# Inverse norms of q and k: from two GpSimd powers per pair to ten Vector instructions in the last product's PSUM bank

## What is computed

```python
qkv = x @ Wqkv                       # 128 -> 3 * 1024, 16 heads of 64
q = l2norm(q) * qs;  k = l2norm(k) * ksc
q = q * cos * scale + rotate_half(q) * sin * scale
k = k * cos / scale + rotate_half(k) * sin / scale
out = local_attention(q, k, v)       # windows of 32 rows, each sees itself and the one before
x = out @ Wo + x                     # then the feed-forward part, in the same manner
```

## Time and profile before

| what | us |
|---|---|
| median of 3 runs | 5035.57 (5034.55 to 5038.77) |
| profiled execution | 5033.9 |
| its span | 5032.1 |
| busy in the span: PE / DVE / ACT / POOL | 4258.0 / 2925.1 / 2870.9 / 3317.2 |
| L915, the power, 192 times | 1044.1 |
| one round (p2, p3, p0, p1 in the stretch 3006.11 to 3173.61) | 39.66 + 38.71 + 50.55 + 38.58 |

### The profile page before, as it was taken

The page is one execution under the profiler, slowest core; times in us unless marked ns, Lnnn a source line. Parts: engine busy times, 40 slices in busy tenths (PEclk is TensorE's granted clock), DMA queues, the critical chain, the costliest instruction groups (busy, mean ns, idle before and its releaser), DMA issues. The chain is left out here.

```text
span 5032.1 us, 165624 instructions
## 1 busy us (share of the span) xinstructions
PE 4258.0 (85%) x68354; PEld 2963.6 (59%) x68806; DVE 2925.1 (58%) x4217; ACT 2870.9 (57%) x4801; POOL 3317.2 (66%) x1514
## 2 busy tenths in 40 slices
PE   5878878688888888888888888888888888888884
PEld 2434444366666666666666666666666666666663
DVE  6565665565655565556555655565556555655564
ACT  2534445356665666666656666666666566655662
POOL 0000000588788888888788888888888888888882
PEclk9988989799999999999999999999999999999997
DMA  0000000222222222222222212222222122212222
GB/s 26 3 14 15 3 15 2 59 55 65 60 53 61 65 60 53 61 65 60 53 61 65 60 53 61 65 60 53 61 65 60 53 61 65 60 53 61 65 60 76
DMA packets 284570, 259.23 MB, mean 52 GB/s; under 512 B 122871, under 2 KB 258508, under 8 KB 271148
## 3 DMA queue, kind: packets, MB, share of 16 engines
q1 hardware_dynamic: 283820, 248.14, 18.3%
HBM read 117.63 MB, written 29.77 MB: 29 GB/s over the span
## 5 line engine op out<-in xcount | busy, mean ns | idle before, releaser
L790 DVE TENSOR_TENSOR products<-bank_d,table 128x1024 f32<-128x1024 f32 x772 | 937.6, 1215 | 787.5 <-ACT sq L606 751.9
L910 POOL TENSOR_TENSOR products<-products 128x2048 f32<-128x2048 f32 x192 | 870.5, 4534 | 373.7 <-DVE products L790 373.6
L915 POOL TENSOR_TENSOR rnorm<-clamped,minus_half 128x32 f32<-128x32 f32 x192 | 1044.1, 5438 | 16.0
L393 PE MATMUL bank_d<-w_qkv,xT 128*128 128x512 f32 x1544 | 832.0, 632 | 9.9 <-DVE products L790 8.5
L606 ACT ACTIVATE sq<-bank_d 128x512 f32<-128x512 f32 x772 | 467.8, 606 | 531.5 <-PE bank_d L393 521.6
L788 DVE TENSOR_REDUCE ss<-sq 128x16 f32<-128x1024 f32 x386 | 469.6, 1217 | 455.4 <-ACT sq L606 455.4
L933 POOL TENSOR_TENSOR qk_rot<-products,rnorm 128x2048 f32<-128x2048 f32 x192 | 695.4, 3622 | 14.9 <-POOL rnorm L915 14.0
L877 POOL MEMSET ident<- 128x128 f32 x1 | 0.2, 205 | 915.2 <-POOLq L1051 915.2
L462 PE MATMUL scores<-kT,qT 64*32 64x64 f32 x24576 | 424.2, 218 | 141.9 <-issue 79.5
L940 POOL TENSOR_TENSOR prob<-prob,inv_sum 128x1024 f32<-128x1024 f32 x192 | 365.0, 1901 | 261.8 <-DVE inv_sum L770 261.8
L435 PE MATMUL bank_a<-ident,qk_rot 128*128 128x128 f32 x3072 | 423.5, 293 | 116.5 <-issue 107.7
(11 more groups left out here) (160 smaller groups left out, 7647.4 us busy)
## 6 DMA issues: line engine op xcount, KB each, us to landing
v_back<-v SPq DMA_DIRECT2D x96, 768.0 KB, 5.4
w_qkv<-in_Wqkv_dram SPq DMA_DIRECT2D x25, 1024.0 KB, 5.0
v_back<-v SPq DMA_DIRECT2D x192, 128.0 KB, 5.5
w_qkv<-in_Wqkv_dram SPq DMA_DIRECT2D x25, 512.0 KB, 5.2
xs<-x_layers SPq DMA_DIRECT2D x194, 64.0 KB, 2.0
w_o<-in_Wo_dram SPq DMA_DIRECT2D x24, 512.0 KB, 5.8
xr<-x_layers SPq DMA_DIRECT2D x96, 128.0 KB, 3.1
x<-x SPq DMA_DIRECT2D x96, 128.0 KB, 1.8
```

What stands on the lines that cost most here:

```text
L393: nc.tensor.matmul(bank[:, :], xT[:, P * a:P * (a + 1)], w_qkv[:, col:col + 512], start=True, stop=True).then_inc(d_filled if i < 8 else a ...
L790: nc.vector.tensor_tensor(products[:, a, head:head + 8, :, :].rearrange("p h r (o d) -> p h r o d", o=2), bank[:, :].rearrange("p (h r d) ...
L910: link(nc.gpsimd.tensor_tensor(products[:, a, :, 0, :], products[:, a, :, 0, :], products[:, a, :, 1, :], ALU.add))
L915: link(nc.gpsimd.tensor_tensor(rnorm[:, a, :], clamped[:, a, :], minus_half[:, :], ALU.pow))
```

## The change

The clamp and the power leave GpSimd. DVE computes all 64 inverse roots of a pair at once, behind the product of chunk 7: a first guess by integer arithmetic on the bits, one step of third order and one Newton step. The intermediate values x, t and u lie in the first 192 columns of the bank that chunk 7 was in, y and w in SBUF. Each of the ten instructions waits for the one before through the semaphore `v_link`, and the first also for the product. `d_free` of chunk 7 is raised by the tenth instruction in place of the product. The last one also waits for `qk_ready` of the pair before, since it overwrites `rnorm`. On POOL `norm_qk(s, 0)` moves from between the two `normalise` to behind both and behind the wait for chunk 7.

```diff
                 head = HEADS * kq + 8 * c
-                nc.vector.tensor_tensor(
+                product = nc.vector.tensor_tensor(
...
-                    ALU.mult).then_inc(d_free, 1)
+                    ALU.mult)
+                if i == 7:
+                    link(product)
+                    inverse_norms(pair, bank).then_inc(d_free, 1)
+                else:
+                    product.then_inc(d_free, 1)
+
+            def inverse_norms(pair, bank):
+
+                x, t, u = (bank[:, 4 * HEADS * k:4 * HEADS * (k + 1)] for k in range(3))
+                y, w = root_y[:, :], root_u[:, :]
+                link(nc.vector.tensor_scalar(x, ss[:, :, :].rearrange("p a h -> p (a h)"), FLT_MAX, 1e-24, ALU.min, ALU.max))
+                link(nc.vector.tensor_scalar(y.bitcast(i32), x.bitcast(i32), -0.5, float(RSQRT_MAGIC), ALU.mult, ALU.add))
+                link(nc.vector.tensor_tensor(t, x, y, ALU.mult))
+                link(nc.vector.tensor_tensor(t, t, y, ALU.mult))
+                link(nc.vector.tensor_scalar(w, t, 0.375, -1.25, ALU.mult, ALU.add))
+                link(nc.vector.tensor_tensor(u, t, w, ALU.mult))
+                link(nc.vector.scalar_tensor_tensor(y, u, 1.875, y, ALU.add, ALU.mult))
+                link(nc.vector.tensor_tensor(t, x, y, ALU.mult))
+                link(nc.vector.scalar_tensor_tensor(t, t, -0.5, y, ALU.mult, ALU.mult))
+
+                if later(pair.n):
+                    dve.wait_ge(qk_ready, 2 * pair.n)
+                return nc.vector.scalar_tensor_tensor(rnorm[:, :, :].rearrange("p a h -> p (a h)"), t, 1.5, y, ALU.add, ALU.mult)
...
-            def inverse_norms(a):
-
-                link(nc.gpsimd.tensor_scalar(clamped[:, a, :], ss[:, a, :], FLT_MAX, 1e-24, ALU.min, ALU.max))
-                link(nc.gpsimd.tensor_tensor(rnorm[:, a, :], clamped[:, a, :], minus_half[:, :], ALU.pow))
...
                     add_products(s, 0)
-                    inverse_norms(0)
                 if runs(back3):
                     normalise_x1(back3)
                 if runs(back1):
                     normalise(back1, 0)
-                if runs(now):
-                    norm_qk(s, 0)
-                if runs(back1):
                     normalise(back1, 1)
                 if runs(now):
                     pool.wait_ge(d_free, chunk_at(now, 7)[1] + 1)
+                    norm_qk(s, 0)
                     if s.p == POS - 1:
                         make_table(s.f + 1)
                     add_products(s, 1)
-                    inverse_norms(1)
                     norm_qk(s, 1)
```

More of the change, by code:

```diff
@@ L148, in local_layers @@
         rnorm = sb("rnorm", [P, 2, 2 * HEADS])
-        clamped = sb("clamped", [P, 2, 2 * HEADS])
-        minus_half = sb("minus_half", [P, 2 * HEADS])
+        root_y = sb("root_y", [P, 4 * HEADS])
+        root_u = sb("root_u", [P, 4 * HEADS])
+        minus_half = sb("minus_half", [P, 2])
         epsilon = sb("epsilon", [P, 2])
@@ L921, in normalise_x1 @@
                 nc.gpsimd.tensor_scalar(neg_mean[:, :], mean_var[:, :, 0], -1.0, 1.0, ALU.mult, ALU.mult)
-                link(nc.gpsimd.tensor_tensor(rstd[:, :], var_eps[:, :], minus_half[:, 0:2], ALU.pow))
+                link(nc.gpsimd.tensor_tensor(rstd[:, :], var_eps[:, :], minus_half[:, :], ALU.pow))
                 for a in range(2):
```

## The result

The changed kernel takes 5230.3 us (median of 4 runs, 5227.6 to 5236.1) against 5037.2 us (4 runs) before: ratio 1.0384, 95% interval [1.0366, 1.0402]. The profiled execution has a span of 5225.5 us, 193.4 us more than before. The forecast was 5166 us, + 132 us, with a range of 5085 to 5240.

The account below looks back on a forecast made before the run. PE's own work and a few waits were taken to bound the kernel. 1.62 + 1.53 + 1.6 + 0.8 = 5.55 us a round, 128 us in 23 rounds, plus 4 us for the first, gave 5166 us; range 5085 to 5240.

Parts of the forecast that it names:

- What bounds the kernel: Whole step: PE's own work and a few waits set the pace; POOL's busy time is worth nothing by itself.
- The power leaves POOL: At p1 to p3 PE's 1.65 us wait for xn goes, but only 0.3 us come through, yT being next.
- The cost D: Ten DVE instructions between the product of chunk 7 and the row sum take 2.65 us, bounds 2.1 to 3.3.
- The choice to add nothing for the bank: The ten instructions on DVE: PSUM source costs no more than SBUF; the skill's table would add 0.6 us.
- The shift of a step: PE's transposes for ph = 1 start later, waiting for prob: 1.62 us at p1, 1.53 p2, 1.6 p3, 1.95 p0.
- p0 and the holes: PE's 2.4 us hole at p0, read as code loading behind v_back: p0 taken as + 0.8 us.
- the lower of the two ends: At p0 the new wait replaces PE's hole and the clock stays up: -2.2 us; the other end is + 1.95.
- The clock: PE's clock falls behind the new wait, 1.7 us each fall: 5330 us if in each step; chance 0.10.
- The table at p3: At p3 the table makes DVE's rotate 0 of the new pair 2.2 us late, 53 us more: 5219; chance 0.09.
- The other side: In three steps of each round PE keeps 0.3 us if the insertion costs below 0.8 us: 5012 us; chance 0.04.

Follow-up runs that it names:

- the experiment with only the ten instructions: Kernel before with the ten instructions added on DVE, result unread, POOL keeping its clamps and powers: 5225.1 us, ratio 1.0390.
- the two held kernels: v_back loaded behind times_v: the kernel before with only that, 4955.3 us; the changed kernel with that and the ten instructions behind the row sum, 4932.2 us.
- without the roots: Changed kernel with one clamp written to rnorm in place of the ten instructions, q and k scaled wrongly: 4989.1 us, ratio 0.9912.

## Why the prediction was right, and where it was short

**What bounds the kernel.** Right. PE's list and its few waits set each step; POOL lost a third of its busy time and this changed nothing in the loop, as the experiment with only the ten instructions shows most plainly. The exception is the first round, which the prediction didn't look at for this: there the kernels without the power on POOL are 10.5 to 11.6 us faster than their partners with it (140.2 against 128.7 and 129.7, 141.5 against 129.9, and 149.7 with only the ten against 138.9 with the change).

**The power leaves POOL.** Right in kind: of the 1.65 us for `xn` most went into the waits for `gate` and `yT`, 0.6 us each. At p1 0.33 us come through without the roots (38.58 to 38.25), 0.17 with them behind the row sum (38.41), and 0.12 between the two held kernels (38.59 to 38.47). So 0.3 us a step is the upper end, and that the two held kernels are 23 us apart doesn't show it, as worked out above.

**The cost D.** 2.65 us foretold, 2.63 measured. The straight line between two rows was as good as the row itself. The choice to add nothing for the bank was off by 0.12 us of the chain.

**The shift of a step.** Right: with `v_back` held the transposes for ph = 1 begin 1.59, 1.50 and 1.58 us later at p1, p2 and p3, against 1.62, 1.53 and 1.6 foretold, and 1.57 at p0 against 1.95. In the sum it is 7.0 us a round, against 1.62 + 1.53 + 1.6 + 1.95 = 6.7 us worked out with the full shift at p0, so 160.5 us in all. That the sums are so near is luck in part, since by steps p1 took 0.6 us more and p3 and p0 together 0.2 us less.

**p0 and the holes.** Here the forecast was short, by 61 us. The step that failed is the one that set this aside for p0 alone. I had seen that `v_back` would be issued at another moment against PE, named it as the likely cause of the hole at p0, and then asked only what this does to p0. There it did what was foretold in kind: p3 and p0 together rose by 0.8 us instead of 2.4. Counted on PE, p3 rose by 1.9 us, about as foretold, and p0 fell by 1.0: its holes in `times_v` went from 2.70 to 1.20 us a round and its mean granted clock from 0.895 to 0.932, so it went part of the way to the lower of the two ends that the prediction kept. But at p1, where there had been no hole, the later transposes and the nearer load put a packet of PE's code 2.9 us behind the issue of `v_back`, and opened one: + 6.3 us instead of + 1.6, a term of 4.7 x 23 = 108 us that the sum doesn't have. Holding the load takes 4.0 of the 4.7 us away. What it had too much of was 1.6 us at p0 and p3, 37 us. With 2 us of p2, and the first round and the two ends of the program, which came 11 to 12 us lower than counted, the difference is the 61 us.

**The rivals.** The clock did not fall behind the wait for `prob` (1.00 at p1 and p2 in the rounds without a long hole); it fell behind the new hole at p1 in some rounds (mean of the step down to 0.93). The table at p3 did make rotate 0 of the new pair late, by 8.77 us of idle time against 5.29, and this did not show in the step. What the prediction did not ask is what the table does to `qk_rot` of tile 1, which POOL makes behind it: at the end of p3 PE now waits for it in 17 of 23 rounds, 2.0 us in the mean of all. It cost nothing to speak of, as a hole of 2.5 us had been at that place before.

**The other side.** The gain that stays was given D below 0.8 us. The same gain is had without touching D, by standing behind the row sum; that is the case that I should have priced beside it.

## What to carry to other kernels

A chain of small instructions is cheap or dear by what stands behind it in its engine's list: look for the first instruction behind it that another engine waits for, take its slack from the trace, and if the chain is longer, move it behind that instruction. Relieving an engine that nobody waits for gives only what the one wait on it gave, less what stands next in line; look apart at the first steps, where the pipeline fills and another engine can be the one that all wait for. And where a change shifts engines against SP, look at the big loads in every step, not only in the step that has a hole already: where a load lies against dense PE code is worth testing by one held wait.

## What the runs showed of the hardware that I had not expected

- PE's dense stretches can run dry while big DMA loads move. Holding the 1 MB load of `v_back` behind `times_v` took 74.0 us of unexplained PE holes to 8.7 in the kernel before and 117.4 to 12.9 in the changed one, 77 and 114 us of time. In the seven traces in which the load is not held, all 213 holes of over 1 us in `times_v` end 1.21 to 1.61 us behind the landing of a 16,384-byte packet of the instruction queue; in the three with the load held there is no such hole. What the load changes is the start of the packet, by 2.5 us at p0 before and 2.9 us at p1 after. That the queue carries PE's code is inferred from its size and from these times, and how the load keeps the packet back isn't shown. The Trainium skill (Runtime: NRT & Kernel Launch, the section on instruction fetch mechanics) has instructions streamed in blocks of 16 KiB over a queue of the engine's own, which the packets agree with, and calls the cost mostly hidden; with a big load beside dense PE code it was not, by 77 and 114 us.
- Where such a load lies against PE decides: `v_back` 0.6 to 0.9 us nearer, and the packet 1.8 us later behind the transposes, turned a step of constantly 38.6 us into one of 41.3 to 48.1 us, of which 1.6 us are the later `prob`.
- The granted PE clock did not answer to the hole at p1 in the same way each round: behind the hole of 2.9 us that ends at 3095.4 it stayed 1.00, behind the one of 3.9 us that ends at 2568.8 it fell to 0.67 and 0.50 in stretches of 2 us; 0.50, the level of 1.2 GHz, lasted 3.4 us. Behind the 2.2 us hole of p0 that ends at 3125.5 before, it fell as well, for 3.4 us.
